# The experts' last product in three parts of high and low halves, in a gated cross-attention block

## The reference, cut to what matters

```python
def _L0_ffn_ref(x, route_w, A, Bw):
    logits = jnp.einsum('bsd,ed->bse', x, route_w)
    topk_v, topk_idx = jax.lax.top_k(logits, 1)
    route_weight = jax.nn.one_hot(topk_idx[..., 0], E, dtype=logits.dtype) * topk_v
    h = jnp.einsum('bsd,erd->bser', x, A)
    wh = route_weight[..., None] * h
    out = jnp.einsum('bser,eor->bso', wh, Bw) * SCALING      # SCALING is 1
...
x = x + jnp.tanh(g_xattn[0]) * _L0_xattn_ref(_layernorm(x), ctx_4096, ctx_4096, mask, wq, wk, wv, wo, 0)
x = x + jnp.tanh(g_ffn[0]) * _L0_ffn_ref(_layernorm(x), L0_ffn_route_w, L0_ffn_A, L0_ffn_Bw)
```

## Time and profile before

| | |
|---|---|
| Median of 3 runs | 1137.26 us (1136.19 to 1138.29) |
| The profiled execution | 1136.03 us, its span 1134.2 us |
| Granted TensorE clock, mean | 0.995 of full speed |
| TensorE matmuls busy | 1101.8 us, 97% |
| VectorE busy | 900.4 us, 79% |
| ScalarE busy | 626.8 us, 55% |
| GpSimd busy | 611.1 us, 54% |
| The experts' last product (L917) | 32 instructions in 16 tiles |

### The profile page before, as it was taken

How to read it: one execution, slowest core, us unless ns; L and a number is a source line. 1 busy time by engine, 2 the same in 40 slices (tenths; PEclk the granted TensorE clock), 3 DMA queues, 4 the chain that set the end, 5 groups by cost and what they waited for, 6 DMA issues and landing times.

```text
span 1134.2 us, 17081 instructions
## 1 busy us (share of the span) xinstructions
PE 1101.8 (97%) x5664; PEld 921.2 (81%) x5664; DVE 900.4 (79%) x1413; ACT 626.8 (55%) x1090; POOL 611.1 (54%) x513
## 2 busy tenths in 40 slices
PE   7999999889999999999999999999999999999997
PEld 6788888678888888888888777888888888888775
DVE  7984748877787878877888999787878887877887
ACT  6462446466666666666666545455555555555441
POOL 4751458777777777777754434344434334334320
PEclk9999999989999999999999999999999999999999
DMA  6869945476464646464459745453535353542201
GB/s 226 275 233 359 341 152 210 140 280 233 149 224 150 224 148 216 159 195 181 153 214 375 236 140 163 145 183 117 196 125 191 115 179 104 175 140 75 75 1 75
DMA packets 93510, 206.27 MB, mean 182 GB/s; under 512 B 8816, under 2 KB 41712, under 8 KB 87536
## 3 DMA queue, kind: packets, MB, share of 16 engines
q1 hardware_dynamic: 93424, 205.18, 53.2%
HBM read 122.31 MB, written 82.84 MB: 181 GB/s over the span
## 4 chain that ended last, share of the span: by engine, by line
PE 64%; DVE 12%; POOL 11%; issue 8%; ACT 4%; DMA 0%; DVEq 0%; POOLq 0%; SPq 0%; ACTq 0%
PE attn L873 20%; PE proj L814 17%; PE score L831 7%; PE attn L766 6%; POOL rot L1624 3%; PE score L766 3%; PE turned L766 3%; POOL wq_s L1599 2%; PE turned L842 2%; PE attn L858 2%; PE attn L860 2%; DVE q_r L1102 1%; DVE q_r L1060 1%; DVE row_sum L1131 1%; DVE wo_s L1055 1%
## 5 line engine op out<-in xcount | busy, mean ns | idle before, releaser
L873 PE MATMUL attn<-wo_s,o_s 128*128 128x512 f32 x1536 | 378.5, 395 | 0.8 <-DVE o_s L1151 0.8
L814 PE MATMUL proj<-xB,wq_s 128*128 128x512 f32 x1344 | 337.2, 394 | 4.1 <-ACT copies L1422 2.2
L873 PEld LDWEIGHTS attn<-wo_s,o_s 128*128 128x128 f32 x1536 | 283.7, 188 | 58.4 <-DVE o_s L1151 1.3
L814 PEld LDWEIGHTS proj<-xB,wq_s 128*128 128x128 f32 x1344 | 253.1, 189 | 58.5 <-ACT copies L1422 2.6
L1624 POOL TENSOR_TENSOR rot<-rot,tab 128x512 f32<-128x512 f32 x112 | 169.9, 1517 | 173.3 <-ACT rot L1401 173.0
L831 PEld LDWEIGHTS score<-k_r,q_r 128*128 128x128 f32 x1024 | 123.5, 192 | 14.8 <-DVE q_r L1065 9.2
L1400 ACT ACTIVATE rot<-q_r 64x512 f32<-64x512 f32 x86 | 54.2, 630 | 144.6 <-DVE q_r L1102 139.9
L831 PE MATMUL score<-k_r,q_r 128*128 128x64 f32 x1024 | 122.9, 273 | 4.5 <-DVE q_r L1065 4.5
L1143 DVE TENSOR_TENSOR p_low<-turned,p_high 64x512 fp32r<-64x512 f32 x128 | 88.0, 688 | 42.3 <-ACT p_high L1438 40.3
L1446 ACT ACTIVATE o_s<-attn 128x512 fp32r<-128x512 f32 x128 | 69.8, 595 | 76.2 <-PE attn L860 76.1
L1065 DVE TENSOR_TENSOR q_r<-q_r,rot 128x512 f32<-128x512 f32 x86 | 89.0, 1035 | 17.1 <-POOL rot L1624 11.8
(11 more groups left out here) (195 smaller groups left out, 1680.6 us busy)
## 6 DMA issues: line engine op xcount, KB each, us to landing
wq_kept<-wq_s SPq DMA_DIRECT2D x16, 1792.0 KB, 6.2
wq_s<-wq_kept SPq DMA_DIRECT2D x16, 1792.0 KB, 8.3
v_kept<-vst SPq DMA_DIRECT2D x64, 256.0 KB, 4.6
v_s<-v_kept SPq DMA_DIRECT2D x128, 128.0 KB, 4.9
wo_kept<-wo_s SPq DMA_DIRECT2D x32, 512.0 KB, 3.7
wo_s<-wo_kept SPq DMA_DIRECT2D x32, 512.0 KB, 5.1
k_kept<-kst SPq DMA_DIRECT2D x32, 256.0 KB, 2.0
wq_raw<-in_wq SPq DMA_DIRECT2D x16, 512.0 KB, 5.7
```

The source lines that it names most:

```text
L814: last = e.matmul(dst[:, :], wq_s[:, b % 2, A, s, kt, :], xB[:, B, mv, kt, :], start=(first and kt == 0 and m == 0), stop=(kt == 1 and m = ...
L873: last = e.matmul(attn[bp][:, :], o_s[:, s, bp, h, :], wo_s[n % WO_SLOTS][:, m, :], start=(h == 0 and i == 0), stop=(h == GROUP - 1 and i ...
```

## The change

`lora_bT` is halved once: the high half by ScalarE at the end of step 27, the low half by VectorE at the end of step 28, into `lora_s`, which lies where `combined` was. For each tile ScalarE's copy of the turned weighted rows becomes the high half, and a new stage "turn weighted" of VectorE subtracts it from the PSUM bank for the low half. The last product is three matmuls of halves. It waits for VectorE's semaphore `weighted_low` in place of ScalarE's `weighted_copied`. So does the release of the bank of the odd tiles. On ScalarE, place 6 goes ahead of the second `q_shift`; on VectorE, ahead of the step's second `add_out`.

```diff
+LORA_SPLIT = 27
+        late_w = sb_at(base + 122880, "late_w", [P, 2, DM], F32R)
+        expert_w = sb_at(base + 126976, "expert_w", [P, 2, DM], F32R)
+        lora_s = sb_at(combined_at, "lora_s", [P, 2, DM], F32R)
+        def weighted_halves(t):
+            here = late_w if t >= HALF_TILES and t % 4 >= 2 else expert_w
+            return [here[:, t % 2, ER + i * P:ER + (i + 1) * P] for i in range(2)]
...
 TensorE, expert():
                     if par and t < HALF_TILES:
-                        drained[score.name] = weighted_copied, t + 1
+                        drained[score.name] = weighted_low, t + 1
                 else:
-                    e.wait_ge(weighted_copied, t + 1)
+                    e.wait_ge(weighted_low, t + 1)
+                    if t == 0:
+                        e.wait_ge(lora_low, 1)
-                    e.matmul(b[:, :], at[:, ER:ER + P], lora_bT[:, :], start=True, stop=True).then_inc(mixed, 1)
+                    halves = weighted_halves(t)
+                    for i, (s, m) in enumerate(SPLIT_PRODUCTS):
+                        last = e.matmul(b[:, :], halves[s], lora_s[:, m, :], start=(i == 0), stop=(i == 2))
+                    last.then_inc(mixed, 1)
 VectorE, expert():
+                elif what == "turn weighted":
+                    e.wait_ge(weighted_high, t + 1)
+                    halves = weighted_halves(t)
+                    e.tensor_tensor(halves[1], b[:, 0:P], halves[0].bitcast(F32), ALU.subtract).then_inc(weighted_low, 1)
 VectorE, a step:
                 between(k, 5)
+                between(k, 6)
                 if k:
                     add_out(k - 1, 1)
-                between(k, 6)
+                if k == LORA_SPLIT + 1:
+                    e.wait_ge(lora_high, 1)
+                    e.tensor_tensor(lora_s[:, 1, :], lora_bT[:, :], lora_s[:, 0, :].bitcast(F32), ALU.subtract).then_inc(
+                        lora_low, 1)
 VectorE, the last steps:
             add_out(k + 2, 0)
             add_out(k + 2, 1)
+            experts("turn weighted", k)
             experts("mix", k)
...
-            for bp in range(PAIRS):
-                add_out(k + 3, bp)
-                expert_norms_begin(tiles_of(k + 3)[bp:bp + 1])
+            add_out(k + 3, 0)
+            expert_norms_begin(tiles_of(k + 3)[:1])
+            experts("turn weighted", k + 1)
+            add_out(k + 3, 1)
+            expert_norms_begin(tiles_of(k + 3)[1:])
             expert_norms_end(tiles_of(k + 3))
             experts("mix", k + 1)
             experts("route", k + 2)
+            experts("turn weighted", k + 2)
             experts("route", k + 3)
             experts("mix", k + 2)
+            experts("turn weighted", k + 3)
             experts("mix", k + 3)
 ScalarE:
-                    e.activation(at[:, ER:ER + P], b_work[:, 0:P], ACT.Copy).then_inc(weighted_copied, 1)
+                    e.activation(weighted_halves(t)[0], b_work[:, 0:P], ACT.Copy).then_inc(weighted_high, 1)
...
                 between(k, 5)
+                between(k, 6)
                 for q in ropes[1]:
                     q_shift(*q)
-                between(k, 6)
...
+                if k == LORA_SPLIT:
+                    e.wait_ge(wq_low, 4 * HEAD_PAIRS_ALL)
+                    e.wait_ge(routed_in, 32)
+                    e.activation(lora_s[:, 0, :], lora_bT[:, :], ACT.Copy).then_inc(lora_high, 1)
```

More of the change, by code:

```diff
@@ L340, in build @@
         v_both = sb("v_both", [P, 2, CHUNK_TILES, DH], F32R)
+        combined_at = cursor[0]
         combined = sb("combined", [P, 4, 2, P])
@@ L390, in build @@
         copied, out_high = sem("copied"), sem("out_high")
-        x1_copied, weighted_copied = sem("x1_copied"), sem("weighted_copied")
+        x1_copied, weighted_high, lora_high = sem("x1_copied"), sem("weighted_high"), sem("lora_high")
         raw_low_v, x_low, q_summed = sem("raw_low_v"), sem("x_low"), sem("q_summed")
@@ L399, in build @@
         weighted, out_ready = sem("weighted"), sem("out_ready")
+        weighted_low, lora_low = sem("weighted_low"), sem("lora_low")
         zeros_set = sem("zeros_set")
```

## The result

| | before | changed |
|---|---|---|
| First comparison, median | 1136.7 us (8 runs, 1135.13 to 1138.29) | 1139.55 us (8 runs, 1138.26 to 1141.6) |
| Ratio, 95% interval | | 1.0029 (1.0020 to 1.0038) |
| Repeated later | 1137.54 us (32 runs) | 1139.34 us (12 runs), 1.0016 (1.0007 to 1.0024) |
| Profiled execution | 1136.03 us | 1141.6 us, span 1139.8 |
| Mean granted clock in it | 0.995 | 0.991 |

A forecast was written before the change was run, and what follows sets the result against it. TensorE led, but VectorE was as full in the expert steps. Terms 0.54 + 0.89 + 0.75 = 2.2 us on the 1137.26 median, rounded up to 1139.6 for second subtractions; range 1137.2 to 1141.5.

The forecast's parts named there:

- The product: Each tile's last product on TensorE: three matmuls taking 0.68 us for 0.86, taken as 0.17 us less a tile.
- The rival by which it doesn't get shorter: Three separate weight loads keep each product at 0.86 us in all; 1.5 us more, 1141.1; chance 0.08.
- The common matrix: End of step 28: GpSimd's multiply holds VectorE's wide subtraction, so step 29's mask comes 0.54 us late.
- Steps 30 to 34: Changes in step length, by VectorE's low halves and shorter products: -0.17, +0.60, +0.03, +0.60 and -0.17 us.
- The forecast that GpSimd's multiply would move past the VectorE add in step 33: ScalarE's later shift delays that multiply, so the add takes 0.68 us instead of 1.79: 1.1 us back on VectorE.
- The tail: Last four steps: 0.75 us late, 0.10 of it at tiles 8 and 9; TensorE waits for tile 14's half.
- The text's mark for it: Sign to look for: the last sum starts 0.76 us later against the last router product.
- The first rival: Same mechanism, partly swallowed by slack at the common matrix or step 33: 1.1 us more, 1138.3; chance 0.25.
- The second rival: TensorE's saving reaches the end if low halves are ready in steps 31 and 33: 2.7 us off, 1134.5; chance 0.10.
- the clock's rival: New waits in steps 31 and 33 or at 1129 bring another low-clock stretch: 1.7 us more, 1141.1; chance 0.12.

The follow-up runs named there:

- the float32 kernel: Changed kernel with all its halving, waits and order, but the product one float32 matmul of the high half and whole common matrix; 1140.17 us, ratio 1.0025.
- The early subtraction: Changed kernel with VectorE's common-matrix subtraction ten microseconds earlier in step 28, before GpSimd begins; 1139.44 us, ratio 1.0018.
- the even-first kernel: Changed kernel with the even tile's low half ahead of the second low-probability subtraction on VectorE in steps 30 to 33; 1137.42 us, ratio 1.0003.
- the shift-first kernel: Changed kernel with ScalarE's second rope shift ahead of the high halves again in steps 30 to 33; 1141.09 us, ratio 1.0036.
- the combined kernel: Changed kernel with earlier common-matrix subtraction, even tile's low half first, and last low halves ahead of tile 13's sum; 1137.3 us, ratio 0.9994.
- tail order: Changed kernel with VectorE making the low halves of tiles 14 and 15 between the sums of tiles 12 and 13; 1139.22 us, ratio 1.0018.
- ScalarE's order alone: Kernel before, with only ScalarE's copy of the turned weighted rows ahead of the second rope shift in steps 30 to 33; 1136.66 us, ratio 0.9995.

## Why the prediction was right

**The product.** 0.17 us a tile was the term; the float32 kernel gives 0.15 to 0.17 for each of the nine products on the path. The rival by which it doesn't get shorter falls.

**The common matrix.** 0.54 was the term, 0.42 came (0.46 with the subtraction moved away). The mechanism was the named one, an end 0.55 us behind GpSimd's (621.68 + 1.69 against 621.54 + 1.28). The size was 0.12 high, because the mask began 0.08 before the subtraction's end and not 0.04 after it. The early subtraction shows the same 0.68 us that the shortest row of its kind had.

**Steps 30 to 34.** Every one within 0.03 us of the forecast. The cause is shown by the even-first kernel for most of it: move one subtraction ahead of the other, and 1.07 of the 1.30 us of steps 31 to 33 come back. For the other 0.23 VectorE's added work is likely and not shown. The forecast that GpSimd's multiply would move past the VectorE add in step 33 was right too, and the shift-first kernel shows its price, 1.11. Without it the change would have cost 3.5 us in its places.

**The tail.** 0.75 was the term for all of it, 0.72 came (0.11 at tiles 8 and 9, 0.61 at 14 and 15). The text has VectorE 0.14 late ahead of tile 14, where its own sum for tiles 8 and 9 is 0.10; with that it would have had 0.72 as well. The text's mark for it, the last sum 0.76 later against the last router product, was wrongly set: tiles 8 and 9 lie ahead of that product, so 0.65 was what the working gives.

**The first rival**, a part of it swallowed, fell: 1.40 of the 1.43 us came in the first distance.

**The second rival**, that TensorE's saving reaches the end, was ruled out for this order. Its condition, halves that are there when TensorE asks, is what the combined kernel makes nearly true, and the time then is 1137.3, not 1134.5: the waits for the weighted rows, 0.85 twice, and 0.52 in the tail stay, and savings ahead of such a wait are lost in it.

**The clock, and luck.** 2.1 us in the places stand against 2.85 and 1.80 over all, so that 1139.6 fell 0.05 from the first median is partly luck. It was reckoned from 1137.26, and the kernel before had 1136.7 in that comparison; and it was rounded up for a pair of subtractions at 0.45 us, which took 0.41 (671.90 to 672.31). The profiled execution had a second low stretch, near 1125, as the clock's rival has one, though not behind a wait that the rival named; none of the eight later profiles had it, and what brought it isn't known. Whether the change lengthens the stretch behind 1074 is open. For it: a mean clock of 0.994 or more stood in 8 of 20 runs of the changed kernel, and in 41 of the 59 of the kernel before that ran beside the experiments. Against it: 14 of those 59 were at 0.992, and the kernel with the float32 product, whose order of work is the changed one's, shows the short stretch and the combined one the long. At an equal mean clock the difference is nearer the places': at 0.994 the means are 1138.75 us for 1136.90 (6 and 21 runs), 1.8 more; at 0.992, 1139.86 for 1138.15 (5 and 14 runs), 1.7 more.

## What to carry to other kernels

- When a product is replaced by cheaper ones on halves, count the engine that makes the halves first. Here TensorE was spared 0.17 us a tile and VectorE took on 0.41 for every two, in steps where TensorE was already waiting for VectorE; even in the best order tried that gained nothing.
- A short instruction that another engine waits for goes ahead of a long one that nobody waits for yet. Three moves, two of this kind and one out of GpSimd's way, gave back the 2 us that the change cost, without any less work.
- Look at what runs on GpSimd when a VectorE instruction with both inputs in SBUF starts. The price of a meeting, about 1 us here, counts only where someone waits for what comes behind it: for the add of step 33, nothing in the kernel before, all of it in the changed one.

## What the runs showed of the hardware that had not been expected

- The stretch at 1.2 GHz behind the same wait near 1074 lasted about 3.4 us in some profiles (the kernel before, even first, float32 product, ScalarE's order alone) and about 6.8 us in others (the changed kernel twice, matrix early, tail order, shift first, all three), behind a wait of TensorE that is 1.3 us long in the kernel before and in the changed one alike. The longer one costs some 1.6 us, more than any single term of this forecast. What decides between them was not found.
- The clock fell once near 1125, in one of ten profiles. TensorE had waited 2.02 us for VectorE's sum just before, and the eight matmuls of its next router product took 2.06 us. In the repeat the same eight, behind a wait of the same 2.02 us, took 1.17, at a granted clock of 1.00.

The profiled changed kernel, and then its repeat:

```profile
1124.38 2.06 PE L920 MATMUL small<-routedT,expert_s 128*128 128x136 f32 x8 [2.02 <-DVE acc L1229]
```

```profile
1124.34 1.17 PE L920 MATMUL small<-routedT,expert_s 128*128 128x136 f32 x8 [2.02 <-DVE acc L1229]
```

A wait that long does not by itself decide whether the clock falls.
